# Pairwise attention over 26 embedding fields: the last quad's last fields in parts, its last three groups in column halves

## The reference, cut to what matters

```python
B, N_DENSE, N_FIELDS, VOCAB, EMBED_DIM, ATT_DIM = (2048, 13, 26, 12500, 32, 8)
FIRST, SECOND = np.triu_indices(N_FIELDS, k=1)              # 325 pairs
emb = rows of 26 tables picked by sparse                    # 2048 x 26 x 32
bi = emb[:, FIRST, :] * emb[:, SECOND, :]                   # 2048 x 325 x 32
a = relu(einsum('bpd,dh->bph', bi, att_w_w) + att_w_b)      # 8 hidden values a pair
scores = einsum('bph,ho->bpo', a, att_d_w) + att_d_b
att_weight = softmax(scores, axis=1)                        # over the 325 pairs
att_out = sum(att_weight * bi, axis=1)
out = sigmoid(concatenate([att_out, dense]) @ fin_w + fin_b)
```

## Time and profile before

| | |
|---|---|
| runs | 483.4, 483.76, 483.77 us; median 483.76 us |
| profiled execution | 483.39 us, its span 481.6 us |
| granted TensorE clock | 0.996 of full speed over the span |
| PE busy | 450.2 us (93%) |
| DVE busy | 372.6 us (77%) |
| POOL busy | 347.9 us (72%) |
| ACT busy | 95.8 us (20%) |

### The profile page before, as it was taken

How to read it: one execution, slowest core, us unless ns; L and a number is a source line. 1 busy time by engine, 2 the same in 40 slices (tenths; PEclk the granted TensorE clock), 3 DMA queues, 4 the chain that set the end, 5 groups by cost and what they waited for, 6 DMA issues and landing times.

```text
span 481.6 us, 6198 instructions
## 1 busy us (share of the span) xinstructions
PE 450.2 (93%) x2280; PEld 177.6 (37%) x2280; DVE 372.6 (77%) x645; ACT 95.8 (20%) x198; POOL 347.9 (72%) x372
## 2 busy tenths in 40 slices
PE   0699999999998999999999899999999899999884
PEld 0354443343333533333333443333334344333221
DVE  6337788796965979799775969879786788887985
ACT  0000101131252011112243101113234201114253
POOL 5777777777777777777777777777777777777740
PEclk9999999999999999999999999999999999999998
DMA  6933743121122223222112222213111222322210
GB/s 221 250 13 15 147 58 36 13 15 13 15 13 15 14 14 79 15 14 14 14 14 13 15 13 15 13 13 15 14 13 16 14 15 13 15 13 14 15 10 1
DMA packets 13661, 15.06 MB, mean 31 GB/s; under 512 B 6368, under 2 KB 12608, under 8 KB 13248
## 3 DMA queue, kind: packets, MB, share of 16 engines
q0 software_dynamic: 11776, 6.05, 23.1%
q1 hardware_dynamic: 1360, 7.53, 4.2%
q10 hardware_dynamic: 496, 1.09, 0.6%
HBM read 14.61 MB, written 0.03 MB: 30 GB/s over the span
## 4 chain that ended last, share of the span: by engine, by line
PE 78%; POOL 8%; DVE 5%; issue 4%; DMA 3%; ACT 1%; POOLq 0%; DVEq 0%
PE looked_own L391 33%; PE back_s L391 16%; PE first L405 13%; PE sums_f L415 12%; POOL emb L368 8%; PE sums_s L429 3%; DVE onehot L667 2%; DMA chunk_numbers<-index_chunk 1%; DMA emb<-tables,rows 1%; DMA chunk_of<-chunk_numbers 1%; PE back_f L442 1%; PE back_s L452 1%; DVE look_masked L678 1%; DMA par<-params 1%; DVE ring L691 0%
## 5 line engine op out<-in xcount | busy, mean ns | idle before, releaser
L368 POOL DMA_INDIRECT emb<-tables,rows x324 | 305.9, 944 | 98.7 <-issue 96.9
L691 DVE TENSOR_TENSOR ring<-emb_t,turned 128x512 f32<-128x512 f32 (+9 forms) x180 | 193.9, 1114 | 3.4
L391 PE MATMUL looked_own<-look_table,onehot 128*128 128x448 f32 x434 | 178.0, 554 | 17.0 <-DVE onehot L667 16.7
L391 PEld LDWEIGHTS looked_own<-look_table,onehot 128*128 128x128 f32 x434 | 79.5, 192 | 114.4 <-issue 114.4
L507 ACT ACTIVATE hidden<-first,par 128x512 f32<-128x512 f32 (+1 forms) x84 | 56.5, 678 | 284.7 <-PE first L405 284.4
L391 PE MATMUL back_s<-look_table,onehot 128*128 128x448 f32 x238 | 94.4, 545 | 3.1 <-DVE score L739 3.1
L405 PE MATMUL first<-ring,par 128*32 128x512 f32 (+1 forms) x672 | 90.7, 591 | 4.3 <-DVE ring L691 4.3
L415 PE MATMUL sums_f<-ring,par 128*32 128x512 f32 (+1 forms) x672 | 90.0, 583 | 0.0
L667 DVE TENSOR_TENSOR onehot<-chunk_of,turned 128x2048 f32<-128x2048 f32 (+1 forms) x24 | 48.3, 2018 | 26.6 <-PE looked_own L391 21.2
L391 PEld LDWEIGHTS back_s<-look_table,onehot 128*128 128x128 f32 x238 | 44.0, 190 | 51.7 <-issue 51.7
L368 POOL DMA_INDIRECT emb<-tables,rows_first x44 | 41.8, 950 | 17.2 <-issue 13.1
(11 more groups left out here) (56 smaller groups left out, 101.0 us busy)
## 6 DMA issues: line engine op xcount, KB each, us to landing
emb<-tables,rows POOLq DMA_INDIRECT x324, 3.2
look_table<-tables SPq DMA_DIRECT2D x3, 1568.0 KB, 8.2
chunk_of<-chunk_numbers SPq DMA_DIRECT2D x3, 768.0 KB, 4.9
chunk_of<-chunk_numbers ACTq DMA_DIRECT2D x1, 768.0 KB, 3.8
emb<-tables,rows_first POOLq DMA_INDIRECT x44, 3.8
par<-params ACTq DMA_DIRECT2D x1, 258.5 KB, 3.1
ids<-sparse SPq DMA_DIRECT2D x1, 208.0 KB, 2.5
feats<-dense SPq DMA_DIRECT2D x1, 104.0 KB, 8.1
```

Of the source, the lines that this page charges most:

```text
L368: pool.indirect_dma_start(emb[:, f, g * D:(g + 1) * D], None, stacked, bass.IndirectOffsetOnAxis(ap=row, axis=0),).then_inc(gathered[f], 16)
L391: mm = nc.tensor.matmul(looked_rows[look_bank[tile]], onehot[:, c, g * P:(g + 1) * P], look_table[:, n, c, :], start=c == 0, stop=c == CHU ...
L691: nc.vector.tensor_tensor(slot[:, at:at + n, :], emb_t[:, i:i + n, :], turned[:, f % 2, :].unsqueeze(1).broadcast_to((P, n, P)), ALU.mult) ...
```

## The change

Most of it is for the last quad (`q == QUADS - 1`).

1. Fields 22 to 25 are cut by tile: fields 22, 23 and 24 in two parts (tiles 0-1, 2-3), field 25 in three (tiles 0-1, tile 2, tile 3). Each part has a semaphore for its gathers; DVE waits for a part, turns its columns, multiplies them by all earlier fields and goes on to the next. Pieces are reported with a field's last part, and those of field 25 also with its first (`pieces_half_done`). The order of the gathers on POOL is unchanged.
2. Groups 18, 19 and 20 are taken in two halves of 64 of the 128 columns of each chunk, by first, relu, final and score products and the copy of the scores.
3. The second full bank is turned back behind group 15 rather than 16: final(15), its scores, `finals_back` and `scores_back` come before first(16), and ACT's copies come before relu(16).
4. In all quads the early maximum is taken bank by bank: 512 elements behind field 20 and 512 behind field 24, then the minimum of the two (negated) results.
5. At the last quad's end ACT and not DVE copies `sums_f`, behind the second half of the scores, and DVE and not ACT copies the end bank's finals home, behind `rise`. `scores_back` comes before the last `final_products_half`.

```diff
+    def cuts_of(q, f):
+        if q < QUADS - 1 or f < CUT_FIELD:          # CUT_FIELD = 22
+            return [slice(0, G)]
+        if f < F - 1:
+            return [slice(0, G // 2), slice(G // 2, G)]
+        return [slice(0, G // 2)] + [slice(g, g + 1) for g in range(G // 2, G)]
+    MAX_FIELDS = (EARLY_FIELD - 4, EARLY_FIELD)
+    def back_at_once(q, gr):
+        return q == QUADS - 1 and gr == FULL * GROUPS_B - 1
 # PE
+                def first_products_half(gr, half):
+                    last = gr - (GROUPS - 3)
+                    if half == 0:
+                        pe.wait_ge(pieces_half_done, last + 1)
+                        if last < 2:
+                            pe.wait_ge(relu_done, q * GROUPS + (gr - 1))
+                        else:
+                            pe.wait_ge(relu_half_done, last - 1)
+                    else:
+                        pe.wait_ge(pieces_done, q * PIECES + pieces_through_group(gr))
+                        if last < 2:
+                            pe.wait_ge(relu_half_done, 3)
+                        else:
+                            pe.wait_ge(relu_done, q * GROUPS + (gr - 1))
 ...
                         first_products(gr)
-                        if gr - 1 in batch_ends:
+                        if gr - 1 in batch_ends and not back_at_once(q, gr - 1):
                             score_products(batch_ends.index(gr - 1))
                         final_products(gr)
-                        if gr and gr % GROUPS_B == 0:
-                            finals_back(gr // GROUPS_B - 1)
-                            scores_back(gr // GROUPS_B - 1)
+                        if back_at_once(q, gr):
+                            score_products(batch_ends.index(gr))
+                        if back_at_once(q, gr) or gr and gr % GROUPS_B == 0 and not back_at_once(q, gr - 1):
+                            finals_back((gr - 1) // GROUPS_B)
+                            scores_back((gr - 1) // GROUPS_B)
 ...
+                if q == QUADS - 1:
+                    score_products(BATCHES - 2)
+                    for gr in range(GROUPS - 3, GROUPS):
+                        first_products_half(gr, 0)
+                    final_products_half(GROUPS - 3, 0)
+                    score_products_half(0)
+                    final_products_half(GROUPS - 2, 0)
+                    final_products_half(GROUPS - 1, 0)
+                    for gr in range(GROUPS - 3, GROUPS):
+                        first_products_half(gr, 1)
+                    final_products_half(GROUPS - 3, 1)
+                    score_products_half(1)
+                    final_products_half(GROUPS - 2, 1)
+                    scores_back(FULL)
+                    final_products_half(GROUPS - 1, 1)
+                    finals_back(FULL)
+                    break
 # ACT, last quad
+                    for half in range(2):
+                        for gr in range(GROUPS - 3, GROUPS):
+                            relu_group_half(gr, half)
+                        copy_scores_half(half)
+                    act.wait_ge(finals_done, (q + 1) * GROUPS)
+                    act.wait_ge(back_f_done, q * BANKS + FULL)
+                    nc.scalar.activation(second_f[:], sums_f[:], ACT.Copy).then_inc(second_f_end_done, 1)
 # DVE
-                    turn_field(f)
-                    dve.wait_ge(transposed, q * F + (f + 1))
-                    for field, a, b in pieces:
-                        if field == f:
-                            pair_products(f, a, b)
+                    for k in range(len(cuts_of(q, f))):
+                        turn_field(f, k)
+                        for field, a, b in pieces:
+                            if field == f:
+                                pair_products(f, a, b, k)
 ...
+                    if f in MAX_FIELDS:
+                        n = MAX_FIELDS.index(f)
+                        dve.wait_ge(score_done, q * FULL + n + 1)
+                        nc.vector.tensor_reduce(neg_max_bank[:, n], score[:, :, n * PAIRS_B:(n + 1) * PAIRS_B], AX.X,
+                                                ALU.max, negate=True).then_inc(bank_max_done, 1)
                     if f == EARLY_FIELD:
-                        dve.wait_ge(score_done, (q + 1) * FULL)
-                        nc.vector.tensor_reduce(neg_max_early[:], score[:, :, 0:EARLY_PAIRS], AX.X, ALU.max,
-                                                negate=True).then_inc(early_max_done, 1)
+                        dve.wait_ge(bank_max_done, (q + 1) * FULL)
+                        nc.vector.tensor_tensor(neg_max_early[:], neg_max_bank[:, 0], neg_max_bank[:, 1], ALU.min
+                                                ).then_inc(early_max_done, 1)
 ... (DVE, last quad, behind rise)
+                    dve.wait_ge(back_f_done, (q + 1) * BANKS)
+                    nc.vector.tensor_copy(pairs_of(final, FULL * GROUPS_B, END_GROUPS - 1), finals_in_bank(end_whole))
+                    end = final[:, :, (GROUPS - 1) * PAIRS_G:].rearrange("p g (c j) -> p g c j", j=COL_TILES)
+                    nc.vector.tensor_copy(end, finals_in_bank(end_last)[:, 0, :, 0:LAST_C, :]).then_inc(final_done, 1)
```

139 lines of the change are left out of this document (110 added, 29 removed).

## The result

The changed kernel takes 486.8 us (median of 6 executions, 485.31 to 489.01) against 483.72 us (6 executions, 483.4 to 483.82): the ratio is 1.0072, interval [1.0045, 1.0099]. It is slower by 3.1 us, and it scatters over 3.7 us where the kernel before scatters over 0.4. The profiled execution is its fastest, 485.31 us with a span of 483.4; against 483.39 and 481.6 before it is 1.9 us longer as an execution and 1.8 in its span. So there are two things to explain: 1.9 us in the traces, and the rest, which is in other executions.

A forecast was written before the change was run, and what follows sets the result against it. The prediction saw a two-sided tail: rows slightly late for DVE, then DVE's field 25 with PE and ACT behind it. 1.25 + 0.1 = 1.35 on the median 483.76 gave 485.1 us, range 482.8 to 486.0.

The forecast's parts named there:

- The steps of the tail: Last quad: predicted start times on DVE, PE and ACT, from field 22 at 453.35 to `scores_back` at 475.86.
- the 1.25: Last quad's end: `scores_back` at 475.86 instead of 474.61, 1.25 us later.
- The end's 0.1: Behind `scores_back`: finals ready at 478.16, DVE copies them until 478.7; 0.1 us taken as felt, bounds 0 and 0.35.
- The sum, 1.35: Whole kernel: 1.25 for the last quad's chain plus 0.1 for the end, added to the execution before.
- The half-wide four at 0.43: PE, groups 18 to 20: four matmuls of half the columns last 0.43 us, a full four 0.86.
- the added maximum at 0.60: DVE behind field 20: the extra 512-element reduce costs 0.53 + 0.07 = 0.60 us, so field 22 begins at 453.35.
- the halves don't shorten the tail: Last quad, groups 18 to 20: DVE's last product to the transposition took 3.4 us with one group open; now three half-groups are.
- The unit cost of a product: DVE: a product of N elements in a row costs N/960 + 0.067 us from start to start.
- The rival in which each pays its whole 0.152: DVE: each short product costs 0.085 us more, DVE ends at 473.5; +1.95, 485.7 us; chance 0.13.
- All waits for rows are gone and are eaten up: DVE, fields 23 to 25: the three waits, 1.8 us together, vanish into added work; DVE ends at 471.55, 0.36 later.
- "other places" step: First three quads: reduce behind field 20 adds 0.60, field 24 saves 0.3; put at 0, between -0.1 and +0.3.
- The rival of the clock: PE: clock falls to 1.2 GHz in the 2.0 us wait ahead of group 15, adding about 2 us: 487; chance 0.03.

The follow-up runs named there:

- the filler: Changed kernel plus six unread 128-column matmuls ahead of the first products of groups 14 and 15, last quad: 486.55 us, ratio 1.0044; later 487.08, 1.0058.
- the edit that gives DVE two waits for rows back: Changed kernel with fields 22 to 24 whole and the second full bank turned back behind first(16) as before: 484.6 us, ratio 1.0003.

## Why the prediction was wrong, point by point

The direction and the mechanism of the tail were right, the size was not: 485.1 foretold, 486.8 measured, above the top of the range, 486.0.

**The steps of the tail held.** The predicted times are in the frame of the execution before; those of after stand here less the 0.36 of the anchor. Field 22 begins at 453.35 (foretold 453.35), first(15) 460.29 (460.32), score 462.17 (462.21), `scores_back` of the second bank 464.04 (464.06), first(16) 464.63 (464.59), first(17) 466.37 (466.32), exponentials 468.06 (468.15), first half of 20 at 470.63 (470.57), scores of the half 471.54 (471.47), DVE's last product ends 471.50 (471.55), scores of the second half 474.82 (474.66), copy 475.51 (475.34), `scores_back` 476.03 (475.86). So the 1.25 came out as 1.42. Of the missing 0.17, 0.07 is there at the first half's scores, and another 0.10 between the relu of 18's second half and first(20), which took 0.62 (473.65 to 474.27) where 0.52 was booked. The end's 0.1 came out as 0.05. The sum, 1.35, was 1.47. The half-wide four at 0.43 was right, and so was the added maximum at 0.60. That the halves don't shorten the tail was half right: with the parts there, taking the halves away costs 0.5 more. The distance from DVE's last product to the transposition did grow, from 3.4 to 4.53 us.

**The unit cost of a product.** N/960 + 0.067 held down to 128 elements: three with 800 elements together take 1.12 = 0.83 + 0.152 + 2 x 0.067, and the three of field 23's second part, 1472 elements, 1.81 where the sum gives 1.82. The rival in which each pays its whole 0.152 is out. By the Trainium skill, "VectorE: DVE Perf Modes", section on the trn2 errata, each small tile would have paid its latency; here the rows decide against it.

**The step that failed: "All waits for rows are gone and are eaten up", and with it the sum, made against one execution and then set against the median ("so against the median I say 483.76 + 1.35 = 485.1").** I booked the three waits of 1.8 us as idle time that the added work may use free of charge. They were also a slack. In the kernel before the end hangs on POOL's gathers, and by the three waits DVE may come up to 1.8 us late with nothing lost. The change spends that slack, so the end hangs on DVE's anchor, and each delay of the start (anchor 449.27 to 451.85 in five traces) arrives whole. The traced execution, with an anchor only 0.36 late, was the least of it: the last one carries 2.56 + 1.47 = 4.03 over the span before, which is all of 485.6 - 481.6 (to rounding). That the kernel before absorbs such a start is inferred, from the gather in its last chain and from the scatter: its 37 executions in the two later sessions lie within 1.9 us (483.16 to 485.04), the 19 of the filler within 4.5, and the edit that gives DVE two waits for rows back lies within 1.3. No trace shows the kernel before with a late start. The "other places" step, 0 with at most +0.3, missed this: it asked what the change adds elsewhere, not what arrives from elsewhere.

**The rival of the clock, given 0.03,** is real, but it sits elsewhere. Of 11 traces of kernels with both long waits and no filler 4 show the fall, all four at the 730 level; of 5 with filler, none. With such counts the traces alone don't prove the filler's effect. The rival named the wait ahead of group 15; the fall comes each time behind the wait of 2.14 ahead of group 14, which the prediction doesn't mention. What it costs depends on how long it lasts: 0 to 0.05 us in three, 1.87 in one, "about 2" as the rival had it. In timed executions at the ordinary level the mean granted clock tells: of the 13 of the unedited changed kernel 6 are at 0.990 or less and take 488.03 on the mean, the other 7 take 486.32. All 19 of the filler lie at 0.996 or above, mean 486.61, against 487.11 for the 13. (Of the 37 later executions of the kernel before one, at 484.59, has 0.990, the others 0.994 and more.) So the clock accounts for some 0.5 to 0.8 us of the mean, and not for most of the miss. What was wrong is the place of the wait and the chance: the longest wait of before (1.62) and the clock of 1.00 beside it were taken as evidence for 2.0, and one trace can't show how often something happens.

**The account.** The mean of the 13 executions is 487.11; the kernel before, in the same two sessions, has 483.9: 3.2 us. The tail is 1.47 of it (traces), the clock 0.5 to 0.8 (timed executions). The remaining 0.9 to 1.2 fit the late anchors, but the traces cover only a part. Against the trace of before the anchors are -0.02, 0.36, 0.76, 1.74 and 2.56 in the five traces of the changed order, 1.1 on the mean; the mean of the kernel before lies itself 0.5 above its trace, so 0.6 is left. The 19 executions with the filler, where the clock is no reason, lie 1.7 above 483.39 + 1.47 + 0.1, so their anchors would have to be 1.7 late on the mean. The split between clock and anchors is not settled, since the intervals of filler and changed kernel overlap ([1.0041, 1.0075] and [1.0041, 1.0081]), and on the one chip that had both the means are 486.77 and 487.08.

**What this doesn't explain.** At the 730 level no row is late in the traces, so no slack is spent there. Still the changed kernel is 2.1 to 6.3 us above the kernel before, more than tail and clock together in most sessions, and the kernel with only field 25 in parts is 1.6 and 2.6 above although its tail is 0.7 shorter. So something ahead of the tail costs time at that level. No trace of the kernel before exists there, and no run isolates it.

**Which version is best.** None beats the kernel before. Whole fields 22 to 24 with the bank turned back later equals it within the interval. Turning the bank back later with the parts kept was only run where rows are early, so its time at the ordinary level is open.

## What to carry to other kernels

Before idle time in front of a transfer is booked as free, ask what arrives late there in other executions: a wait that absorbs the scatter of another chain is worth the mean of what it absorbs. Look at several traces of the same kernel and measure the end from both chains; the distance that stays the same names what sets it. Do it within one kernel only: between two kernels an equal distance can be chance. And when a piece is reported later, so that TensorE waits longer than anywhere in the trace before, price the fall of its clock at more than a few per cent, and try a few idle matmuls in the wait.

## What the runs showed of the hardware

- The first look-up starts at 16.3 to 16.6 us in five of the seven traces of the ordinary level and at 18.3 to 18.4 in two, because two small transfers in a row each take 0.8 to 0.9 us longer; the first 14 look-ups then take 7.45 to 8.52. Both together, 2.56 us between kernel before and last trace, are more than the whole change of the tail, 1.47.
- The granted clock fell to 0.50 in 4 of 11 traces, each time at group 14's products behind a wait of 2.14 us. With six small matmuls ahead of group 14 and of group 15 it stayed at 1.00 there in 5 of 5.
- Transposing half as many columns on DVE takes 0.25 instead of 0.32 us (`turned`) and 0.20 instead of 0.27 (`emb_t`), a quarter 0.22: the fixed part is most of it.
- All these kernels took about 484 to 488 us on some chips and 730 to 740 on others, with the same tail to 0.05 us where the clock didn't fall. What stalls it there stays open.
